# Splitting the first weight transfer in three and loading ScalarE's first table set at its start, in a fused attention and recurrence kernel

## The reference

```
h = concat([ctx, x], axis=1)
q = x @ q_w + q_b;  k, v = split(h @ kv_w + kv_b)
a = softmax(where(mask, q @ k.T / DH, -inf));  y = (a @ v) @ out_w + out_b + x
out = gelu(rmsnorm(y) @ mlp_w1 + mlp_b1) @ mlp_w2 + mlp_b2 + x
```

## Time and profile before

| What | Value |
|---|---|
| median of 3 runs | 1046.31 us (1045.92 to 1046.83) |
| time of the profiled execution | 1047.43 us |
| its span in the profile | 1045.6 us |
| PE busy | 971.0 us, 93% of the span |
| ACT busy, table loads | 752.8 us, 126 loads |
| PE's first matmul | 7.45 us |
| first scores on PE | 18.51 us |

### The profile page before, as it was taken

One profiled execution on the slowest core, in us unless ns is written; L12 is line 12 of the kernel. 1 busy time (PEld: TensorE's weight loads), 2 busy tenths in 40 slices (PEclk: granted clock), 3 DMA queues, 4 the chain that ended last, 5 costly groups with the idle time before them and its releaser, 6 DMA issues.

```text
span 1045.6 us, 18911 instructions
## 1 busy us (share of the span) xinstructions
PE 971.0 (93%) x6760; PEld 742.4 (71%) x6760; DVE 717.1 (69%) x1275; ACT 752.8 (72%) x2031; POOL 483.1 (46%) x391
## 2 busy tenths in 40 slices
PE   5879989999999999999999999999999999979554
PEld 3666757777787777777787777777787777767333
DVE  1345767777686867677686867678686867776662
ACT  4465677877888787877888787877888787864521
POOL 1105444635446354635446354635446354643440
PEclk9798999999999999999999999999999999989776
DMA  7104224060604224060704225060604225050500
GB/s 278 38 0 75 45 49 71 25 104 1 121 9 85 44 58 72 18 112 1 120 9 85 45 57 72 13 117 1 120 10 84 46 57 73 23 81 3 82 18 10
DMA packets 37116, 60.91 MB, mean 58 GB/s; under 512 B 10464, under 2 KB 13088, under 8 KB 36896
## 3 DMA queue, kind: packets, MB, share of 16 engines
q1 hardware_dynamic: 37024, 59.72, 31.4%
HBM read 21.95 MB, written 4.19 MB: 25 GB/s over the span
## 4 chain that ended last, share of the span: by engine, by line
PE 86%; DVE 6%; ACT 3%; issue 2%; POOL 2%; DMA 1%; POOLq 0%; SPq 0%; DVEq 0%; ACTq 0%
PE psum L375 38%; PE psum L476 11%; PE psum L393 6%; PE psum L438 5%; PE psum L400 4%; PE psum L424 3%; PE psum L380 3%; PE psum L546 3%; PE psum L450 3%; DVE tmp L898 2%; PE psum L506 2%; PE psum L556 2%; PE psum L494 2%; POOL xm L972 1%; PE psum L552 1%
## 5 line engine op out<-in xcount | busy, mean ns | idle before, releaser
L989 POOL TENSOR_TENSOR rs<-st,rr 128x512 f32<-128x512 f32 x128 | 188.3, 1481 | 265.1 <-DVE st L920 253.0
L964 POOL TENSOR_TENSOR probs<-probs,rsum 128x512 f32<-128x512 f32 x128 | 146.0, 1141 | 205.6 <-DVE rsum L809 204.2
L621 ACT ACTIVATE probs<-psum,neg_max 128x128 f32<-128x128 f32 x512 | 180.7, 398 | 19.7 <-DVE neg_max L804 19.4
L593 ACT ACT_TABLE_LOAD x126 | 161.7, 1283 | 2.3
L920 DVE TENSOR_TENSOR_SCAN st<-decay,kv 128x512 f32<-128x512 f32 x128 | 156.2, 1232 | 0.2
L375 PE MATMUL psum<-xm,w_sb 128*128 128x256 f32 x512 | 125.1, 393 | 1.6 <-POOL xm L972 1.0
L621 ACT ACTIVATION_READ_ACCUMULATOR probs<-psum,neg_max 128x1 f32 x512 | 121.6, 238 | 0.0
L375 PEld LDWEIGHTS psum<-xm,w_sb 128*128 128x128 f32 x512 | 96.7, 194 | 31.8 <-issue 15.9
L375 PE MATMUL psum<-y,w_sb 128*128 128x256 f32 x512 | 117.2, 388 | 2.2 <-DVE y L837 2.2
L476 PE MATMUL psum<-hid,w_sb 128*128 128x256 f32 x512 | 113.1, 379 | 0.0
L375 PEld LDWEIGHTS psum<-y,w_sb 128*128 128x128 f32 x512 | 97.7, 193 | 19.0 <-issue 3.0
(11 more groups left out here) (116 smaller groups left out, 1664.8 us busy)
## 6 DMA issues: line engine op xcount, KB each, us to landing
vb<-vr SPq DMA_DIRECT2D x128, 256.0 KB, 7.4
h_sb<-hT SPq DMA_DIRECT2D x16, 512.0 KB, 4.2
xa_sb<-xT SPq DMA_DIRECT2D x16, 256.0 KB, 4.2
out<-x SPq DMA_DIRECT2D x16, 256.0 KB, 4.4
mask_i<-maskT SPq DMA_DIRECT2D x16, 128.0 KB, 4.4
w_sb<-W SPq DMA_DIRECT2D x2, 768.0 KB, 7.0
w_sb<-W SPq DMA_DIRECT2D x1, 1280.0 KB, 9.5
w_sb<-W SPq DMA_DIRECT2D x1, 1248.0 KB, 13.3
```

The source lines that it names most:

```text
L593: sc.preload_act_table_set(table)
L621: last = fn(probs[:, u % PROBS, n, :], bank(g, f"s{u}")[:, n * P:(n + 1) * P], ACT.Exp, bias=neg_max[:, u % PROBS, n:n + 1], accum_out=sum ...
L964: tt(probs[:, u % PROBS, :, :], probs[:, u % PROBS, :, :], rsum[:, u % PROBS, :].unsqueeze(2).broadcast_to([P, 4, KEYS]), ALU.mult).then_i ...
L989: tt(rs[:, (RH * g + n) % RS, :], st[:, n % 2, :], flat(rr), ALU.mult).then_inc(rs_made.sem, 1)
```

## The change

The transfer of the q, k and v columns becomes three, with the tokens `h` between the first and the second and `VEC` behind the second. PE waits for each part by its own semaphore. ACT loads the table set of exponentials and logarithms as its first instruction, and the kernel's bookkeeping starts from that set.

```
-W_PARTS = (("q", "v"), ("o", "w1"), ("maa1", "Wg"), ("Wfk", "Wfv"))
+W_PARTS = (("q", "q"), ("o", "w1"), ("maa1", "Wg"), ("Wfk", "Wfv"), ("k", "k"), ("v", "v"))
-SP_ORDER = """3:spread 0:h 4:store 0:mask 0:load0 1:s0 1:xa 0:row0 3:row1 0:load1"""
+SP_ORDER = """3:spread 0:h 0:loadk 0:loadv 4:store 0:mask 0:load0 1:s0 1:xa 0:row0 3:row1 0:load1"""
-ONCE = ("bias", "load0", "load1", "fold0", "fold1", "fold2")
+ONCE = ("bias", "loadk", "loadv", "load0", "load1", "fold0", "fold1", "fold2")
@@ SP, piece_of
+                elif piece == "loadk":
+                    load_weights(4)
+                    sp.dma_start(vec[:, :], VEC[:, :]).then_inc(ld_vec.sem, 16)
+                elif piece == "loadv":
+                    load_weights(5)
@@ SP, ahead of its list
-            sp.dma_start(vec[:, :], VEC[:, :]).then_inc(ld_vec.sem, 16)
             load_weights(0)
@@ PE, piece_of
                 if piece in ("q", "k0", "k1", "v0", "v1"):
                     if g == 0:
-                        pe.wait_ge(ld_w[0].sem, 16)
+                        pe.wait_ge(ld_w[{"q": 0, "k": 4, "v": 5}[piece[0]]].sem, 16)
@@ ACT
-            loaded = [None]
+            loaded = [LEARNT]
+            sc.preload_act_table_set(LEARNT)
```

More of the change, by code:

```diff
@@ L67 @@
 3:mean1 2:td2 1:bias 1:va1 0:k0 3:var1 1:o 0:q 0:k1 1:rms 0:v0 0:sc0 1:w0 1:w1 1:w2 1:w3 1:c0 1:c1 1:c2 1:c3 2:ga0 2:G 1:mean0"""
-ACT_ORDER = """1:ex7 2:K 2:R 1:pt5 1:ev0 3:row1 1:pt7 2:e1 3:sq1 1:ev1 2:decay 3:lnr1 1:ysq 0:qt 0:kt1 0:kt0 1:lna 0:vv0 3:sh1 0:ex0 0:ex1 1:ge0 1:ge1
-1:ge2 1:ge3 0:ex2 0:ex3 2:G 1:sq0 1:lnr0 3:relu 1:sh0 3:tr 1:first 1:th 0:pt1 2:gsq 2:lng 0:row0
-1:tw 0:vv1 2:gu 0:ex4 1:V 0:pt3 0:ex5 0:ex6"""
+ACT_ORDER = """1:ex7 2:K 2:R 1:pt5 1:ev0 3:row1 1:pt7 2:e1 3:sq1 1:ev1 2:decay 3:lnr1 1:ysq 0:qt 0:kt1 0:kt0 1:lna 0:vv0 3:sh1 0:ex0 0:ex1 1:ge0 1:ge1 1:ge2 1:ge3
+0:ex2 0:ex3 2:G 1:sq0 1:lnr0 3:relu 1:sh0 3:tr 1:first 1:th 0:pt1 2:gsq 2:lng 0:row0 1:tw 0:vv1 2:gu 0:ex4 1:V 0:pt3 0:ex5 0:ex6"""
 DVE_ORDER = """2:ysum 4:nm1 3:kv2 3:st1 2:yn 3:st2 1:mx0 1:mx1 3:kv3 4:sx1 3:kv4 4:xf0 4:xf1 3:st3 3:st4 3:kv5 1:mx2 1:mx3 3:st5 3:kv6 2:fold1 3:kv7 1:in0 2:fold2
@@ L246, in build @@
         ld_vec, ld_mats, ld_w2, ld_small, ld_j = (Event(n, 0) for n in ("vec_in", "mats_in", "w2_in", "small_in", "by_j_in"))
-        ld_w = [Event(f"weights_in{i}", 0) for i in range(4)]
+        ld_w = [Event(f"weights_in{i}", 0) for i in range(len(W_PARTS))]
         fills, folded = Event("fills", 0), Event("folded", 0)
```

## The result

The changed kernel took 1040.88 us (median of 9 runs, 1038.72 to 1043.99) against 1046.83 us before (9 runs, 1044.85 to 1048.27). The ratio is 0.9949, with a 95% interval of 0.9934 to 0.9965, 5.3 us by the ratio and 5.9 by the medians: more than twice the 2.3 that were forecast, and outside the range on record (1042.9 to 1045.3).

The account below looks back on a forecast made before the run. PE sets the pace from turn 2, and turn 0's chain from the first transfer to the scores shifts all later work. -1.28 (load) and -1.06 (transfers) give -2.34, from 1046.31 to 1043.97 us; range 1042.9 to 1045.3.

Parts of the forecast that it names:

- Term 1, the load: Turn 0, ahead of `qt`: ACT's table load hides under the first transfers, so the scores come 1.28 us earlier.
- The second load: ACT's load at 18.77, ahead of the first exponential: its removal is worth nothing, since ACT idled 0.46 us after it.
- Term 2, the transfers: Start of turn 0: k lands at 6.20 or 6.30 instead of tokens at 7.31, so PE starts 1.06 us earlier.
- The rival of slow 1 KB rows: First transfers: 1 KB rows slow the queue, k lands 5.24 us later, total 1050.3 us; chance 0.05.
- The sum at the scores: First scores of turn 0: load and transfers together bring them 2.34 us earlier, to near 16.2.
- the paragraph on the clock: Turn 0 onward: the rise follows PE's start on the mean; later low-clock pauses, unchanged in length, cost nothing.
- by a step: Slow-clock stretches up to 88 us: one longer or shorter could cancel the gain or double it; no chance given.
- The rival of the unmoved rise: PE's `k0` and `q`: the clock's rise stays near 12.9, transfers gain only 0.54, time 1044.5 us; chance 0.2.
- That of the rise caught earlier: PE's `q`: the earlier start makes four slow pieces fast, 0.86 us more, time 1043.1 us; chance 0.1.

Follow-up runs that it names:

- e2: Only the transfers split, ACT's table loads left as in the kernel before: median 1045.3 us, ratio 0.9986 to the kernel before.
- e9: Changed kernel with two extra table loads on ACT ahead of the first exponential, delaying PE's restart: median 1045.3 us.
- e7: Changed kernel with small matmuls filling two PE pauses, ahead of the first transposes and the first `va`: median 1039.3 us.
- e10: Kernel before with 14 small matmuls behind the wait for the first rsum, so PE resumes earlier: median 1043.3 us, ratio 0.9973.
- e1: Kernel before with only ACT's table load moved to its start, transfers unchanged: median 1043.7 us, ratio 0.9975.
- e3: Kernel before, run again unchanged: median 1046.5 us.
- e5: Kernel before with 20 small matmuls in PE's idle gap ahead of the first scores: median 1045.8 us, ratio 0.9994.
- e6: Changed kernel with 48 small matmuls ahead of `k0`, while PE waits for the first transfers (warm start): median 1041.7 us.
- e8: Changed kernel with small matmuls at the start, in two pauses and in three later pauses: 1034.6 us.
- e11: Kernel before with small matmuls at the start, in two pauses and in three later pauses: median 1036.8 us.
- e12: Changed kernel with small matmuls at the start and in five pauses, run a second time: median 1035.96 us.
- e4: Changed kernel with SP's first transfer held back by a scratch fill on DVE: median 1044.7 us.

## Why the prediction was wrong

- *Term 1, the load, 1.28.* Right as a mechanism: the load runs at 0.73 us, ACT has left the chain, the scores follow `v0` in 0.02 us. The second load cost nothing, as said: ACT idles 1.39 us at that place where it idled 0.46.
- *Term 2, the transfers, 1.06.* Right: k landed at 6.31 (6.20 and 6.30 forecast), PE started 1.09 us earlier, and e2 alone gave 1.5 us (0.4 to 2.5 by its interval) with an unchanged clock. The rival of slow 1 KB rows is out.
- *The sum at the scores* was 2.69 instead of 2.34: `q` took 2.21 us instead of 2.58, since the clock rose after fewer of its pieces. This part is luck of the execution: with PE's start within 0.2 us of the changed kernel's, the scores came at 15.26 in e9 and at 15.92 in e7, by where the rise fell.
- *The step that failed* is the paragraph on the clock: "these pauses aren't changed in length, so I cost them at nothing". The lengths indeed aren't changed (3.85 us ahead of the first transposes in both), but the length doesn't decide alone. The clock's fall stands at a distance from its rise (10.2 us in each of the ten traces in which it falls in this pause), the rise hangs on PE's start, and the load's removal took 1.28 us out of the distance from start to restart. In both traces of the kernel before, PE came back after the fall (0.65 and 0.24 us), and the clock was low for 6.8 us, over the transposes and `v1`; in the changed kernel's it came back 0.28 ahead of it, and the clock was up again after 3.4. That this holds for most of the other executions is worked out from their clocks, not seen in traces. What follows (`va`, `bias`, `k0` of group 1) then shifts too, and the later low stretches were shorter in the profiled execution. Over all runs this came to some 3 us on top of 2.3. e9 and e10 show the step from both sides: the distance made 1.1 us longer cost 3.7, and PE back earlier with nothing else moved gave 2.8.
- That a stretch could come out longer or shorter "by a step" and "double" the gain stood in the last paragraph, as a thing that makes me wrong; it was put down as scatter of both signs, and carried no chance. It had one sign.
- *The rival of the unmoved rise* is out: with PE's start at 7.3 to 7.7 us the rise came at 10.4 to 13.4 (before, e1, e3, e5, e10), with a start at 6.2 to 6.4 at 9.1 to 11.3 (after, e2, e7, e9), and with one at 1.1 near 6.2 to 7.0 (e6, e8, e11, e12). That of the rise caught earlier fits the profiled pair (4.63 us behind the start instead of 5.31), but by luck: the distance scatters from execution to execution. Its size, 0.86 us at `q`, left out what the clock does later.

Open stays by how much each of the later stretches (31 to 47 and 65 to 88 us) is bound to the first. The second and third were 10.2 and 13.7 us long in before, e2, e5, e6, e9 and e10, and 3.4 and 10.2 in after and e1; but e3, with a long first stretch, has 3.4 and 13.7, and e4, with a short one, 3.4 and 17.1. I have one profile for each kernel, and the split of the 3 us over the three stretches isn't measured.

## What to carry to other kernels

Where PE's clock falls in a pause, look at where PE restarts against the fall, and not only at the length of the pause: an edit worth 1.3 us on the chain was worth 2.9 here (0.9 to 4.3 by its interval), with the restart ahead of the fall. An edit that shifts start and restart together (the split) showed no such bonus, and one that moves the rise alone (the warm start) can lose its gain in the next pause. Where pauses of PE cannot be removed, small matmuls into a free bank hold the clock, and were worth 6 us here, more than the change; and before a change is judged by a difference under 1%, its runs are compared at an equal granted clock.

## What the runs showed of the hardware

- A table load is 1.28 us with nothing behind it: in the kernel before `qt` began 0.01 us after its end, and in e9 two loads in a row (15.88 and 17.17) were followed by the first exponential at 18.46. The drain of 1.38 us in the Trainium skill's page "ScalarE: Activation LUTs", section "What ACT_TABLE_LOAD costs", shows in no trace here.
- A delay inside a pause of PE can cost three times its length: e9's 1.1 us cost 3.7 on the mean.
- The mean granted clock of a run goes with its time within one kernel: in e1, 6 runs at 0.961 had a mean of 1046.0, 3 runs at 0.968 one of 1040.5.
- The Trainium skill's page "TensorE: Matmul & The Clock Gate", section "Part 1: The HAM clock gate", says that the meter runs free of the kernel's start and makes the rise vary from run to run. The traces agree: in the kernel before the rise came 5.3 us after PE's start (7.45 and 12.8) and in e3, the same kernel, 6.1 us after it (7.25 and 13.4), and the scatter of 5 us in the changed kernel's runs goes with the clock. The page puts the ramp at under 1% of a kernel. The size agrees and still matters: the clock made 0.3 of the 0.5% that the change brought.
